# Mixing in a decoder block: epsilon, power, shift and store made per four tiles, the shift on VectorE

## The chip, the cores and the metric

The kernel runs on one core of a Trainium2 chip. The metric is device time of one execution in microseconds (us). Its engines are TensorE (PE, with its weight loads shown apart as PEld), VectorE (DVE), ScalarE (ACT), GpSimd (POOL) and SyncE (SP, which here only issues DMAs). Each engine runs its own instructions in order, and they wait for each other by semaphores.

## The reference, cut to what matters

The kernel is a decoder block on 64 sequences of 128 tokens with 128 features, all in float32: attention, cross attention and a soft mixture of experts, each followed by a residual and a layer normalisation. The change lies in the last part, where every token mixes the outputs of 64 experts with 32 slots each by a softmax over the experts.

```python
def _layernorm(x, axis=-1, eps=1e-05):
    m = jnp.mean(x, axis=axis, keepdims=True)
    v = jnp.var(x, axis=axis, keepdims=True)
    return (x - m) / jnp.sqrt(v + eps)
...
    logits = (jnp.einsum('tzd,ed->tze', x, phi_w) + phi_b).reshape(t, z, n, p)
    C = jax.nn.softmax(logits, axis=2)
    ...
    Y = jnp.einsum('tznp,npH->tzH', C, Y_tilde)
    return Y
...
x = _layernorm(x + _L0_ffn_ref(x, L0_ffn_phi_w, L0_ffn_phi_b, L0_ffn_expert_w, L0_ffn_expert_b), axis=-1)
```

## The kernel before

The program runs in blocks one after the other: setup, attention, cross attention, gathering the slots, the experts, and mixing. Mixing (mix_slots, L1261) begins at about 950 us of the span and lasts until its end. It handles 64 tiles of 128 tokens. The weights C of one tile are 128 tokens by 2048 (64 experts by 32 slots); they are made in two units of 1024 columns. For one tile:

- PE makes the logits of the first unit from six matmuls (L1200). Those of the second were kept in DRAM by an earlier block, and SP loads them into mix_read (L1192).
- DVE finds the largest logit per slot, of the first unit (mix_mx, L1227) and of the second (mix_high, L1231), and lowers one half of the first unit in PSUM (L1236); PE lowers its other half (L1206); POOL lowers the second unit (mix_less, L1249).
- ACT takes the exponentials of the first unit (L1215) and of the second (L1219). DVE sums each (mix_sums, L1241) and inverts the sums (mix_rinv, L1244). POOL multiplies each unit by them (mix_c, L1256).
- PE turns each unit (last_T, L1331), ACT copies it out of PSUM (last_cT, L1340), PE multiplies it with the slots' outputs (last_Y, L1324).
- The normalisation: DVE adds the residual (last_y, L1364) and takes mean and variance (L1367 to L1370); POOL adds epsilon, takes the power -0.5 and makes the shift, minus mean times the result (L1387, L1390, L1392), one column each; ACT makes the output, last_res, from y by this scale and shift (L1349); SP stores the outputs of two tiles with one DMA (L1304).

The order is written out by hand: every engine steps through k in ORDER, two steps to a tile, and a stage with lag n handles tile (k - n) / 2 in step k. In an even step DVE sums the second unit of one tile, finds the peaks of a later one and lowers it. In an odd step it does its part of the normalisation of the tile with lag 7 and then sums the first unit of the tile with lag 1. POOL divides two units in an even step and lowers one in an odd step, and then makes the three small values of the tile with lag 7. Two buffers of each kind are held in turn. reach() is a wait that is left out where its value is not above zero.

Of the kernel before, what the change touches and what calls it, by code (L numbers as in the profile page):

```python
# [55 lines left out]
def reach(eng, sem, value):  # L56

    if not isinstance(value, int) or value > 0:
        eng.wait_ge(sem, value)  # L59
# [1201 lines left out]
def mix_slots(nc, w, mix, out):  # L1261
# [5 lines left out]
    with ExitStack() as ctx:  # L1267
        st = Store(nc, ctx, "last")
        cT = [st.sb(f"cT{i}", [128, 8, 128]) for i in range(2)]
        y = [st.sb(f"y{i}", [128, 128]) for i in range(2)]  # L1270
        stats = st.sb("stats", [128, 6])
        mv = [st.sb(f"mv{i}", [128, 2]) for i in range(2)]
        veps = st.sb("veps", [128, 1])
        rstd = [st.sb(f"rstd{i}", [128, 1]) for i in range(2)]
        shift = [st.sb(f"shift{i}", [128, 1]) for i in range(2)]
        res = [st.sb(f"res{i}", [128, 2, 128]) for i in range(2)]
# [17 lines left out]
        ORDER = range(UNITS + 9)  # L1294

        @block.sync
        def _(sync):
            for t in range(TILES + 4):
                if t + READS - 1 < TILES:
                    mix.load(sync, t + READS - 1)  # L1300
                if t >= 4 and t % 2 == 0:
                    p = (t - 4) // 2
                    sync.wait_ge(res_ready, 2 * p + 2)
                    sync.dma_start(out[p * 256:(p + 1) * 256, :].rearrange("(b s) d -> s b d", b=2), res[p % 2][:])\  # L1304
                        .then_inc(stored[p % 2], 16)
            for i in range(2):
                sync.wait_ge(stored[i], 16 * (TILES // 4))
# [27 lines left out]
        def _(act):  # L1335
            for k in ORDER:
# [8 lines left out]
                for t in tiles(k, 8):  # L1345
                    act.wait_ge(shift_ready, t + 1)
                    if t >= 4:
                        act.wait_ge(stored[t // 2 % 2], 16 * (t // 4))
                    act.activation(res[t // 2 % 2][:, t % 2, :], y[t % 2][:], ACT.Identity, bias=shift[t % 2][:],  # L1349
                                   scale=rstd[t % 2][:]).then_inc(res_ready, 1)  # L1350

        @block.vector
        def _(dve):
            for k in ORDER:
# [3 lines left out]
                for t in tiles(k, 0):  # L1358
                    if t >= EARLY:
                        mix.peaks(dve, t)  # L1360
                for t in tiles(k, 7):
                    dve.wait_ge(cT_read, 2 * t + 2)
                    reach(dve, res_ready, t - 1)
                    dve.tensor_tensor(y[t % 2][:], psY[t % 2][:, 0:128], w.xres[:, t * 128:(t + 1) * 128], ALU.add)\  # L1364
                        .then_inc(y_done, 1)
                    dve.wait_ge(y_done, t + 1)
                    dve.bn_stats(stats[:], y[t % 2][:]).then_inc(st_done, 1)  # L1367
                    dve.wait_ge(st_done, t + 1)
                    dve.memset(w.scratch[:], 0.0)
                    dve.bn_aggr(mv[t % 2][:], stats[:]).then_inc(mv_ready, 1)  # L1370
# [5 lines left out]
        def _(pool):  # L1376
            for k in ORDER:
# [7 lines left out]
                for t in tiles(k, 7):  # L1385
                    pool.wait_ge(mv_ready, t + 1)
                    pool.tensor_tensor(veps[:], mv[t % 2][:, 1:2], w.eps[:, 0:1], ALU.add).then_inc(ve_done, 1)  # L1387
                    pool.wait_ge(ve_done, t + 1)
                    reach(pool, res_ready, t - 1)
                    pool.tensor_tensor(rstd[t % 2][:], veps[:], w.neg_half[:, 0:1], ALU.pow).then_inc(rstd_ready, 1)  # L1390
                    pool.wait_ge(rstd_ready, t + 1)
                    pool.tensor_scalar(shift[t % 2][:], mv[t % 2][:, 0:1], -1.0, rstd[t % 2][:], ALU.mult, ALU.mult)\  # L1392
                        .then_inc(shift_ready, 1)
# [104 lines left out]
```

## Time and profile before

| | us |
|---|---|
| median of 3 runs | 1399.61 (1399.18 to 1403.23) |
| the profiled execution's own time | 1401.92 |
| its span | 1399.9 |
| POOL busy in the span | 1180.2 (84%) |
| DVE busy | 1109.3 (79%) |
| PE busy, PE weight loads busy | 1293.0 (92%), 1055.0 (75%) |
| ACT busy | 896.6 (64%) |
| the chain that ended last: mix_c L1256, mix_less L1249 | 14%, 5% of the span |
| the same chain: last_rstd, last_shift, last_veps | 2%, 1%, 1% |

The span is that of one execution taken by the profiler, 2.0 us shorter than this execution's own time, which in turn is 2.3 us above the median. The shares are averages over all blocks. In the part of the span that mixing takes, the granted clock of PE is full, and PE, DVE and POOL are all busy for nine tenths or more, so that shares alone do not tell which of them sets the pace.

### The profile page before, as it was taken

How to read it: one execution, taken by the hardware profiler on the slowest of the kernel's cores; microseconds unless marked ns; L12 is line 12 of the kernel's file. 1: busy time of each engine (PE TensorE's matmuls, PEld its weight loads, DVE VectorE, ACT ScalarE, POOL GpSimd, SP SyncE). 2: the span in 40 equal slices, each digit the busy share in tenths (PEclk: the TensorE clock that was granted, in tenths of full speed). 3: DMA queues.
4: the chain of work that ended last, by engine and by line, in shares of the span. 5: the costliest groups of instructions: out<-in, count | busy, mean ns of one | idle time of the engine just before them, and what ended most of it. 6: DMA issues, size and time to landing. Idle time of an engine off the chain costs nothing. (4 is left out here: it accounts for less than half of the span.)

```text
span 1399.9 us, 31677 instructions
## 1 busy us (share of the span) xinstructions
PE 1293.0 (92%) x11006; PEld 1055.0 (75%) x11006; DVE 1109.3 (79%) x2462; ACT 896.6 (64%) x1670; POOL 1180.2 (84%) x1050
## 2 busy tenths in 40 slices
PE   4886789999999699999999999979999999999998
PEld 3664567777676477777777777748999999999997
DVE  4897456666666688888888888877999999999996
ACT  2897356666666476776776777735666666666664
POOL 7664568888888399999999999967999999999997
PEclk9998699999999999999999999999999999999999
DMA  5111243443443022222222222212222223232321
GB/s 167 47 40 55 84 134 117 121 122 115 125 121 94 24 84 89 92 83 91 91 84 90 91 87 87 84 48 94 84 88 83 88 84 89 82 91 80 92 79 31
DMA packets 83567, 123.61 MB, mean 88 GB/s; under 512 B 8593, under 2 KB 54226, under 8 KB 83410
## 3 DMA queue, kind: packets, MB, share of 16 engines
q1 hardware_dynamic: 81810, 117.16, 26.4%
q0 software_dynamic: 1088, 4.19, 1.0%
q8 instruction: 90, 1.47, 0.4%
q14 instruction: 67, 0.55, 0.1%
q10 hardware_dynamic: 512, 0.23, 0.1%
HBM read 70.28 MB, written 51.27 MB: 87 GB/s over the span
## 5 line engine op out<-in xcount | busy, mean ns | idle before, releaser
L997 POOL TENSOR_TENSOR gather_d<-gather_e,gather_rinv 128x1024 f32<-128x1024 f32 x128 | 244.8, 1913 | 36.6 <-DVE gather_rinv L976 36.5
L1256 POOL TENSOR_TENSOR mix_c<-mix_e,mix_rinv 128x1024 f32<-128x1024 f32 x128 | 240.9, 1902 | 18.7 <-DVE mix_rinv L1244 16.6
L1324 PEld LDWEIGHTS last_Y<-kept_phi,last_cT 128*128 128x128 f32 x2048 | 248.4, 192 | 7.3
L1324 PE MATMUL last_Y<-kept_phi,last_cT 128*128 128x128 f32 x2048 | 249.0, 275 | 0.0
L1340 ACT COPY last_cT<-last_T 128x1024 f32<-128x1024 f32 x128 | 128.4, 1003 | 132.1 <-PE last_T L1331 132.1
L822 POOL TENSOR_TENSOR cross_kd<-first_pack,kept_consts 128x624 fp32r<-128x624 f32 x128 | 155.6, 1237 | 63.7 <-DMA first_pack<-first_halves 54.1
L730 DVE TENSOR_REDUCE cross_mx<-cross_S 128x8 fp32r<-128x624 f32 x128 | 103.5, 809 | 113.0 <-PE cross_S L567 113.0
L1241 DVE TENSOR_REDUCE mix_sums<-mix_e 128x16 f32<-128x1024 f32 x128 | 155.8, 1217 | 34.4 <-ACT mix_e L1215 34.0
L972 DVE TENSOR_REDUCE gather_rsum<-gather_e 128x32 f32<-128x1024 f32 x128 | 156.1, 1220 | 25.9 <-ACT gather_e L945 25.9
L991 POOL TENSOR_TENSOR gather_dl<-gather_d,gather_dh 128x512 fp32r<-128x512 f32 x128 | 166.5, 1301 | 0.0
L934 ACT COPY gather_keep<-gather_L 128x256 f32<-128x256 f32 x256 | 94.7, 370 | 96.2 <-PE gather_L L908 95.9
L1331 PE MATMUL last_T<-kept_consts,mix_c 128*128 128x128 f32 x1024 | 134.2, 274 | 3.2 <-POOL mix_c L1256 1.1
L945 ACT ACTIVATE gather_e<-gather_L 128x1024 f32<-128x1024 f32 x128 | 131.1, 1024 | 7.5
L661 ACT ACTIVATE cross_pT<-cross_P 77x1024 f32<-77x1024 f32 x128 | 131.2, 1028 | 2.1 <-PE cross_P L587 2.1
L922 PE MATMUL slots_X<-gather_d,kept_xres 128*128 128x512 f32 x256 | 130.7, 592 | 0.0
L1249 POOL TENSOR_TENSOR mix_less<-mix_read,mix_high 128x1024 f32<-128x1024 f32 x64 | 122.5, 1914 | 7.4 <-DVE mix_high L1231 4.3
L1331 PEld LDWEIGHTS last_T<-kept_consts,mix_c 128*128 128x128 f32 x1024 | 114.6, 142 | 4.5 <-issue 2.5
L966 DVE TENSOR_REDUCE gather_mx<-gather_L 128x16 fp32r<-128x512 f32 x128 | 88.5, 691 | 30.3 <-PE gather_L L908 21.4
L927 PE MATMUL slots_X<-gather_dh,gather_x2h 128*128 128x512 f32 x128 | 101.0, 789 | 3.0 <-POOL gather_dl L991 3.0
L957 ACT CAST gather_dh<-gather_d 128x512 fp32r<-128x512 f32 x128 | 79.5, 621 | 31.6 <-PE slots_X L929 19.7
L968 DVE TENSOR_REDUCE gather_mx<-gather_L 128x16 fp32r<-128x512 f32 x128 | 87.0, 680 | 0.0
L908 PE MATMUL gather_L<-over_w1h,kept_xh 128*128 128x512 f32 x256 | 81.5, 400 | 4.3 <-ACT gather_e L945 3.3
(205 smaller groups left out, 3013.0 us busy)
## 6 DMA issues: line engine op xcount, KB each, us to landing
kept_logits<-gather_keep SPq DMA_DIRECT2D x128, 256.0 KB, 2.0
mix_read<-kept_logits SPq DMA_DIRECT2D x64, 512.0 KB, 3.7
first_halves<-first_qk SPq DMA_DIRECT2D x32, 412.0 KB, 3.0
first_pack<-first_halves SPq DMA_DIRECT2D x64, 128.0 KB
first_pack<-first_halves SPq DMA_DIRECT2D x32, 206.0 KB
first_pack<-first_halves SPq DMA_DIRECT2D x64, 78.0 KB
attn_xTg<-in_xT SPq DMA_DIRECT2D x16, 256.0 KB, 2.6
kept_xres<-in_x POOLq DMA_DIRECT2D x4, 1024.0 KB, 12.1
```

Of the source, the lines that this page charges most:

```text
L661: act.activation(pT[n % 2][0:J, hs, :, :], psP[:, hs, :, :], ACT.Exp)\
L822: pool.tensor_tensor(kd[n % 2][:, q], keys[:, q].to_broadcast([128, 2, 4, JP]), w.own.unsqueeze(1).unsqueeze(3).to_broadcast([128, 2, 4, J ...
L922: pe.matmul(psX[:, 2 * j + 1, :], w.xres[:, rows(u)], dd[u % 4][:, 1, :], start=first, stop=last)\
L945: act.activation(e[u % 2][:], psL[u % 2][:].rearrange("p i (n s) -> p i n s", n=16), ACT.Exp)\
L972: dve.tensor_reduce(rsum[u % 2][:].rearrange("p (i n) -> p i n", i=2), e[u % 2][:], X, ALU.add)\
L991: pool.tensor_tensor(dl[u % 2][:], dd[u % 4][:, 0, :], dh[u % 2][:], ALU.subtract).then_inc(dl_ready, 1)
L997: pool.tensor_tensor(dd[u % 4][:].rearrange("p i (n s) -> p i n s", n=16), e[u % 2][:], rinv[u % 2][:].rearrange("p (i n) -> p i n", i=2). ...
L1241: dve.tensor_reduce(self.sums[u % 2][:], self.e[u % 2][:], X, ALU.add).then_inc(self.sum_done, 1)
L1256: pool.tensor_tensor(self.cc[u % 2][:], self.e[u % 2][:], self.rinv[u % 2][:].unsqueeze(2).to_broadcast([128, 16, EXPERTS]), ALU.mult)\
L1324: ins = pe.matmul(psY[t % 2][:, 0:128], cT[u % 2][:, c, :], w.yk[:, 8 * (u % 2) + c, :], start=(u % 2 == 0 and c == 0), stop=(u % 2 == 1 a ...
L1331: ins = pe.transpose(psT[:, c, :], mix.cc[u % 2][:, 2 * c:2 * c + 2, :], w.ident)
L1340: act.copy(cT[u % 2][:], psT[:]).then_inc(cT_ready, 1)
```

## The change

The normalisation's small values are made once per four tiles. y, mean and variance of four tiles are collected in one of three buffers. POOL adds epsilon and takes the power on four columns, once in four tiles, and makes no shift. DVE makes the shift on four columns with one instruction, a scalar_tensor_tensor of mean and rstd, two steps after the power. ACT makes the outputs with lag 16 instead of 8. SP stores four tiles with one DMA.

```diff
--- before.py
+++ after.py
@@ -1267,13 +1267,13 @@
     with ExitStack() as ctx:
         st = Store(nc, ctx, "last")
         cT = [st.sb(f"cT{i}", [128, 8, 128]) for i in range(2)]
-        y = [st.sb(f"y{i}", [128, 128]) for i in range(2)]
+        y = [st.sb(f"y{i}", [128, 4, 128]) for i in range(3)]
         stats = st.sb("stats", [128, 6])
-        mv = [st.sb(f"mv{i}", [128, 2]) for i in range(2)]
-        veps = st.sb("veps", [128, 1])
-        rstd = [st.sb(f"rstd{i}", [128, 1]) for i in range(2)]
-        shift = [st.sb(f"shift{i}", [128, 1]) for i in range(2)]
-        res = [st.sb(f"res{i}", [128, 2, 128]) for i in range(2)]
+        mv = [st.sb(f"mv{i}", [128, 4, 2]) for i in range(3)]
+        veps = st.sb("veps", [128, 4])
+        rstd = [st.sb(f"rstd{i}", [128, 4]) for i in range(3)]
+        shift = [st.sb(f"shift{i}", [128, 4]) for i in range(3)]
+        res = [st.sb(f"res{i}", [128, 4, 128]) for i in range(2)]
         psT = st.ps("T", [128, 8, 128])
         psY = [st.ps(f"Y{i}", [128, 512]) for i in range(2)]
 
@@ -1291,20 +1291,24 @@
 
             return [(k - lag) // 2] if (k - lag) % 2 == 0 and 0 <= k - lag < UNITS else []
 
-        ORDER = range(UNITS + 9)
+        def fours(k, lag):
+
+            return [t // 4 for t in tiles(k, lag) if t % 4 == 3]
+
+        ORDER = range(UNITS + 15)
 
         @block.sync
         def _(sync):
-            for t in range(TILES + 4):
+            for t in range(TILES + 12):
                 if t + READS - 1 < TILES:
                     mix.load(sync, t + READS - 1)
-                if t >= 4 and t % 2 == 0:
-                    p = (t - 4) // 2
-                    sync.wait_ge(res_ready, 2 * p + 2)
-                    sync.dma_start(out[p * 256:(p + 1) * 256, :].rearrange("(b s) d -> s b d", b=2), res[p % 2][:])\
+                if t >= 12 and t % 4 == 0:
+                    p = (t - 12) // 4
+                    sync.wait_ge(res_ready, 4 * p + 4)
+                    sync.dma_start(out[p * 512:(p + 1) * 512, :].rearrange("(b s) d -> s b d", b=4), res[p % 2][:])\
                         .then_inc(stored[p % 2], 16)
             for i in range(2):
-                sync.wait_ge(stored[i], 16 * (TILES // 4))
+                sync.wait_ge(stored[i], 16 * (TILES // 8))
 
         @block.tensor
         def _(pe):
@@ -1342,12 +1346,13 @@
                     if t >= 1:
                         mix.exponentials(act, t, 0)
                         mix.exponentials(act, t, 1)
-                for t in tiles(k, 8):
-                    act.wait_ge(shift_ready, t + 1)
-                    if t >= 4:
-                        act.wait_ge(stored[t // 2 % 2], 16 * (t // 4))
-                    act.activation(res[t // 2 % 2][:, t % 2, :], y[t % 2][:], ACT.Identity, bias=shift[t % 2][:],
-                                   scale=rstd[t % 2][:]).then_inc(res_ready, 1)
+                for t in tiles(k, 16):
+                    p, i = t // 4, t % 4
+                    if i == 0:
+                        act.wait_ge(shift_ready, p + 1)
+                        reach(act, stored[p % 2], 16 * (p // 2))
+                    act.activation(res[p % 2][:, i, :], y[p % 3][:, i, :], ACT.Identity, bias=shift[p % 3][:, i:i + 1],
+                                   scale=rstd[p % 3][:, i:i + 1]).then_inc(res_ready, 1)
 
         @block.vector
         def _(dve):
@@ -1358,16 +1363,21 @@
                 for t in tiles(k, 0):
                     if t >= EARLY:
                         mix.peaks(dve, t)
+                for p in fours(k, 9):
+                    dve.wait_ge(rstd_ready, p + 1)
+                    dve.scalar_tensor_tensor(out=shift[p % 3][:], in0=mv[p % 3][:, :, 0], scalar=-1.0, in1=rstd[p % 3][:],
+                                             op0=ALU.mult, op1=ALU.mult).then_inc(shift_ready, 1)
                 for t in tiles(k, 7):
+                    p, i = t // 4, t % 4
                     dve.wait_ge(cT_read, 2 * t + 2)
-                    reach(dve, res_ready, t - 1)
-                    dve.tensor_tensor(y[t % 2][:], psY[t % 2][:, 0:128], w.xres[:, t * 128:(t + 1) * 128], ALU.add)\
+                    reach(dve, res_ready, 4 * (p - 2))
+                    dve.tensor_tensor(y[p % 3][:, i, :], psY[t % 2][:, 0:128], w.xres[:, t * 128:(t + 1) * 128], ALU.add)\
                         .then_inc(y_done, 1)
                     dve.wait_ge(y_done, t + 1)
-                    dve.bn_stats(stats[:], y[t % 2][:]).then_inc(st_done, 1)
+                    dve.bn_stats(stats[:], y[p % 3][:, i, :]).then_inc(st_done, 1)
                     dve.wait_ge(st_done, t + 1)
                     dve.memset(w.scratch[:], 0.0)
-                    dve.bn_aggr(mv[t % 2][:], stats[:]).then_inc(mv_ready, 1)
+                    dve.bn_aggr(mv[p % 3][:, i, :], stats[:]).then_inc(mv_ready, 1)
                 for t in tiles(k, 1):
                     if t >= 1:
                         mix.invert_sums(dve, 2 * t)
@@ -1382,15 +1392,12 @@
                 for t in tiles(k, 1):
                     if t >= 1:
                         mix.lower(pool, t)
-                for t in tiles(k, 7):
-                    pool.wait_ge(mv_ready, t + 1)
-                    pool.tensor_tensor(veps[:], mv[t % 2][:, 1:2], w.eps[:, 0:1], ALU.add).then_inc(ve_done, 1)
-                    pool.wait_ge(ve_done, t + 1)
-                    reach(pool, res_ready, t - 1)
-                    pool.tensor_tensor(rstd[t % 2][:], veps[:], w.neg_half[:, 0:1], ALU.pow).then_inc(rstd_ready, 1)
-                    pool.wait_ge(rstd_ready, t + 1)
-                    pool.tensor_scalar(shift[t % 2][:], mv[t % 2][:, 0:1], -1.0, rstd[t % 2][:], ALU.mult, ALU.mult)\
-                        .then_inc(shift_ready, 1)
+                for p in fours(k, 7):
+                    pool.wait_ge(mv_ready, 4 * p + 4)
+                    pool.tensor_tensor(veps[:], mv[p % 3][:, :, 1], w.eps[:, 0:4], ALU.add).then_inc(ve_done, 1)
+                    pool.wait_ge(ve_done, p + 1)
+                    reach(pool, res_ready, 4 * (p - 2))
+                    pool.tensor_tensor(rstd[p % 3][:], veps[:], w.neg_half[:, 0:4], ALU.pow).then_inc(rstd_ready, 1)
 
 
 class Weights:
```

On POOL, in the middle of mixing, the program before has this order for two tiles; last_veps, last_rstd and last_shift are the three small values, mix_c the two products, mix_less the lowered unit.

```order
L1256 TENSOR_TENSOR mix_c<-mix_e,mix_rinv 128x1024 x2
L1249 TENSOR_TENSOR mix_less<-mix_read,mix_high 128x1024
L1387 TENSOR_TENSOR last_veps<-last_mv,kept_eps 128x1
L1390 TENSOR_TENSOR last_rstd<-last_veps,kept_neg_half 128x1
L1392 TENSOR_SCALAR last_shift<-last_mv,last_rstd 128x1
L1256 TENSOR_TENSOR mix_c<-mix_e,mix_rinv 128x1024 x2
L1249 TENSOR_TENSOR mix_less<-mix_read,mix_high 128x1024
```

And the changed program, over four tiles:

```order
L1249 TENSOR_TENSOR mix_less<-mix_read,mix_high 128x1024
L1397 TENSOR_TENSOR last_veps<-last_mv,kept_eps 128x4
L1400 TENSOR_TENSOR last_rstd<-last_veps,kept_neg_half 128x4
L1256 TENSOR_TENSOR mix_c<-mix_e,mix_rinv 128x1024 x2
L1249 TENSOR_TENSOR mix_less<-mix_read,mix_high 128x1024
L1256 TENSOR_TENSOR mix_c<-mix_e,mix_rinv 128x1024 x2
L1249 TENSOR_TENSOR mix_less<-mix_read,mix_high 128x1024
L1256 TENSOR_TENSOR mix_c<-mix_e,mix_rinv 128x1024 x2
L1249 TENSOR_TENSOR mix_less<-mix_read,mix_high 128x1024
L1256 TENSOR_TENSOR mix_c<-mix_e,mix_rinv 128x1024 x2
L1249 TENSOR_TENSOR mix_less<-mix_read,mix_high 128x1024
```

Three of four tiles have no small values on POOL any more; in the fourth there are two instead of three, of four columns.

On DVE, between the lowering of the first unit (slots_X) and the sum of the next first unit (mix_sums), the program before has:

```order
L1231 TENSOR_REDUCE mix_high<-mix_read 128x16
L1236 TENSOR_TENSOR slots_X<-slots_X,mix_mx 128x512
L1364 TENSOR_TENSOR last_y<-last_Y,kept_xres 128x128
L1367 BN_STATS last_stats<-last_y 128x6
L1369 MEMSET kept_scratch 128x1
L1370 BN_AGGR last_mv<-last_stats 128x2
L1241 TENSOR_REDUCE mix_sums<-mix_e 128x16
L1244 RECIPROCAL mix_rinv<-mix_sums 128x16
```

The changed program has there, once in four tiles:

```order
L1231 TENSOR_REDUCE mix_high<-mix_read 128x16
L1236 TENSOR_TENSOR slots_X<-slots_X,mix_mx 128x512
L1368 SCALAR_TENSOR_TENSOR last_shift<-last_mv,last_rstd 128x4
L1374 TENSOR_TENSOR last_y<-last_Y,kept_xres 128x128
L1377 BN_STATS last_stats<-last_y 128x6
L1379 MEMSET kept_scratch 128x1
L1380 BN_AGGR last_mv<-last_stats 128x2
L1241 TENSOR_REDUCE mix_sums<-mix_e 128x16
L1244 RECIPROCAL mix_rinv<-mix_sums 128x16
```

The new last_shift stands ahead of last_y, so it comes right behind the lowering; in the other three tiles the order is as before.

On ACT, at the end of the program, before:

```order
L1215 ACTIVATE mix_e<-slots_X 128x1024
L1219 ACTIVATE mix_e<-mix_less 128x2x16x32
L1340 COPY last_cT<-last_T 128x1024
L1349 ACTIVATE last_res<-last_y,last_shift,last_rstd 128x128
L1340 COPY last_cT<-last_T 128x1024 x2
L1349 ACTIVATE last_res<-last_y,last_shift,last_rstd 128x128 x3
```

And changed:

```order
L1215 ACTIVATE mix_e<-slots_X 128x1024
L1219 ACTIVATE mix_e<-mix_less 128x2x16x32
L1344 COPY last_cT<-last_T 128x1024
L1354 ACTIVATE last_res<-last_y,last_shift,last_rstd 128x128
L1344 COPY last_cT<-last_T 128x1024 x2
L1354 ACTIVATE last_res<-last_y,last_shift,last_rstd 128x128 x7
```

Seven outputs instead of three stand behind the last copy; the last four of them wait for one shift.

## Rows read from the trace of the kernel before

**Rows 1.** Waits, 960 to 1385 us: us in total, times, longest us.

```profile
DVE mix_sums L1241 <- ACT mix_e L1215: 28.6, 62, 1.7
...
POOL mix_c L1256 <- DVE mix_rinv L1244: 10.7, 46, 1.9
```

**Rows 2.** Timeline, DVE, two tiles: start, us, instruction, idle before it.

```profile
1242.82 0.28 DVE L1364 TENSOR_TENSOR last_y<-last_Y,kept_xres 128x128 f32<-128x128 f32 x1
...
1244.08 1.22 DVE L1241 TENSOR_REDUCE mix_sums<-mix_e 128x16 f32<-128x1024 f32 x1 [0.44 <-ACT mix_e L1215]
1245.33 0.25 DVE L1244 RECIPROCAL mix_rinv<-mix_sums 128x16 f32<-128x16 f32 x1
1245.59 1.22 DVE L1241 TENSOR_REDUCE mix_sums<-mix_e 128x16 f32<-128x1024 f32 x1
...
1249.82 0.28 DVE L1364 TENSOR_TENSOR last_y<-last_Y,kept_xres 128x128 f32<-128x128 f32 x1
...
1251.08 1.22 DVE L1241 TENSOR_REDUCE mix_sums<-mix_e 128x16 f32<-128x1024 f32 x1 [0.43 <-ACT mix_e L1215]
```

**Rows 3.** Timeline, POOL, the same two tiles.

```profile
1238.77 3.76 POOL L1256 TENSOR_TENSOR mix_c<-mix_e,mix_rinv 128x1024 f32<-128x1024 f32 x2 [0.23 <-DVE mix_rinv L1244]
1242.50 1.91 POOL L1249 TENSOR_TENSOR mix_less<-mix_read,mix_high 128x1024 f32<-128x1024 f32 x1
1244.37 0.18 POOL L1387 TENSOR_TENSOR last_veps<-last_mv,kept_eps 128x1 f32<-128x1 f32 x1
...
1245.67 3.76 POOL L1256 TENSOR_TENSOR mix_c<-mix_e,mix_rinv 128x1024 f32<-128x1024 f32 x2
1249.39 1.92 POOL L1249 TENSOR_TENSOR mix_less<-mix_read,mix_high 128x1024 f32<-128x1024 f32 x1
```

**Rows 4.** Timeline, ACT, the two exponentials of one tile.

```profile
1243.02 1.03 ACT L1215 ACTIVATE mix_e<-slots_X 128x1024 f32<-128x1024 f32 x1 [0.15 <-DVE slots_X L1236]
1244.50 1.06 ACT L1219 ACTIVATE mix_e<-mix_less 128x1024 f32<-128x1024 f32 x1 [0.45 <-POOL mix_less L1249]
```

**Rows 5.** Timeline, DVE and POOL together, early in attention.

```profile
18.13 6.95 POOL L214 MEMSET kept_xl<- 32x8192 f32 x1
...
21.05 4.32 DVE L352 TENSOR_SCALAR attn_band<-attn_a 128x512 f32<-128x512 f32 x1 [1.31 <-ACT attn_a L325]
```

**Rows 6.** One line, L352: shortest, median and longest duration in ns.

```profile
L352 DVE TENSOR_SCALAR attn_band<-attn_a x16: 426/427/4315, 21.0 to 118.4; 128x512 f32<-128x512 f32 x16
```

**Rows 7.** Timeline, the last tiles of gathering.

```profile
909.60 1.28 POOL L991 TENSOR_TENSOR gather_dl<-gather_d,gather_dh 128x512 fp32r<-128x512 f32 x1
...
912.98 1.45 POOL L991 TENSOR_TENSOR gather_dl<-gather_d,gather_dh 128x512 fp32r<-128x512 f32 x1
...
913.08 0.23 DVE L982 TENSOR_TENSOR gather_x2l<-kept_xres,gather_x2h 128x128 fp32r<-128x128 f32 x1
```

**Rows 8.** Timeline, POOL: epsilon and power on four columns, in the experts.

```profile
930.72 0.20 POOL L1082 TENSOR_TENSOR expert_veps<-expert_mv,kept_eps 128x4 f32<-128x4 f32 x1 [1.18 <-DVE expert_mv L1044]
931.00 1.01 POOL L1084 TENSOR_TENSOR expert_rstd<-expert_veps,kept_neg_half 128x4 f32<-128x4 f32 x1
```

**Rows 9.** One line, L231: the power on four columns in attention, ns.

```profile
L231 POOL TENSOR_TENSOR attn_rstd<-attn_veps,kept_neg_half x16: 1006/1408/1427, 44.4 to 134.4; 128x4 f32<-128x4 f32 x16
```

**Rows 10.** Timeline, the last tile: power and output.

```profile
1395.53 0.55 POOL L1390 TENSOR_TENSOR last_rstd<-last_veps,kept_neg_half 128x1 f32<-128x1 f32 x1
...
1396.47 0.49 ACT L1349 ACTIVATE last_res<-last_y,last_shift,last_rstd 128x128 f32<-128x128 f32 x1 [3.92 <-POOL last_shift L1392]
```

**Rows 11.** Timeline, attention: shift on DVE and four outputs on ACT.

```profile
135.46 0.16 DVE L361 SCALAR_TENSOR_TENSOR attn_shift<-attn_mv,attn_rstd 128x4 f32<-128x4 f32 x1 [1.39 <-POOL attn_rstd L231]
135.66 1.65 ACT L309 ACTIVATE kept_xres<-attn_y,attn_shift,attn_rstd 128x128 f32<-128x128 f32 x4 [2.48 <-DVE attn_shift L361]
```

**Rows 12.** DMA issues: KB each, median us from issue to landing.

```profile
kept_logits<-gather_keep SPq DMA_DIRECT2D x128, 256.0 KB, 2.0
...
out<-last_res SPq DMA_DIRECT2D x32, 128.0 KB, 1.8
```

## The prediction

> **What bounds the kernel now.** I read the page first. Its chain that ended last runs along POOL, through the divisions, the lowering and the three small values, and POOL is the busiest engine of mixing after PE. Taken by itself that says: take work off POOL and the tile gets shorter. So I went to the waits of mixing and then to the timelines of two tiles in its middle. DVE waits for the first exponential 62 times, 28.6 us in all, and POOL's division waits for DVE's reciprocal in 46 places [rows 1]. In the timelines a tile lasts 6.90 or 7.00 us in turn: the divisions start at 1238.77 and 1245.67 [rows 3], the first sums at 1244.08 and 1251.08 [rows 2].
>
> Where the profile names no wait before a division (1245.67), DVE's reciprocal ended at 1245.33 + 0.25 = 1245.58, 0.09 before it [rows 2, 3]. So POOL had nothing to start earlier with there either; its small values end just in time. What closes the loop is DVE with ACT: DVE lowers the first unit, ACT takes 1.03 us for the exponential from 1243.02 [rows 4], DVE sums it from 1244.08 (1243.02 + 1.03 = 1244.05), inverts, sums the second unit, finds the peaks, lowers the next. In this loop DVE idles 0.43 to 0.44 us a tile and only there [rows 2]; that idle time does not depend on POOL. A second loop, over two tiles, does pass POOL: the reciprocal, two divisions (3.76), mix_less (1.91), the second exponential from 1244.50 for 1.06 to 1245.56, the second sum at 1245.59 [rows 2 to 4]. It delays every second tile by about 0.1, which makes the turn of 6.90 and 7.00. The small values are no part of it either: they stand behind mix_less and ahead of the division, in time that POOL has while it waits for the reciprocal.
>
> **What the change removes.** On POOL, three small values in three tiles of four. From the start of veps to the division they take 1245.67 - 1244.37 = 1.30 us [rows 3]. By the reading above the division still starts 0.09 behind the reciprocal, so this buys nothing in time: after it POOL waits longer for DVE. In the fourth tile POOL has two instructions of four columns: 0.28 from the start of veps to the power, 1.01 for the power [rows 8], and some 0.1 to the division, 1.39 against 1.30. I take the 1.01 of the experts; in attention the power took up to 1.41 [rows 9], where DVE instructions ran beside it. The division then comes 0.1 later once in four tiles (0.5 with 1.41), and half of the tiles have 0.1 to spare. I count it with the next term.
>
> SP's stores, half as many, wait for outputs that are made later, and no longer stand ahead of a load that could be issued. Nothing waits for those loads now, so this is nothing. ACT's outputs keep their place in the even step, behind the copy; the shift they need is made a step before, so nothing too. y and its statistics go to a larger buffer, same instructions. The outputs that free a buffer of y are done some four tiles before it is written again.
>
> **What it adds: the shift on DVE.** It takes 0.16 us [rows 11], once in four tiles, and stands right behind the lowering and ahead of y. Behind it on DVE are y, the statistics and then the first sum, which has the 0.44 of idle time in front. If the shift just ran, 0.16 would vanish in 0.44. But look at what POOL does at that place: mix_less runs from 1242.50 to 1244.41, and y starts at 1242.82, in the next tile from 1249.39 to 1251.31 and at 1249.82 [rows 2, 3]. The shift falls 0.32 to 0.43 behind the start of a POOL instruction that streams 1024 elements a partition out of SBUF. It has two operands in SBUF, mean and rstd. The DVE instructions that stand beside POOL's divisions and mix_less now (the reductions, the lowering in PSUM, y from PSUM and the residual, the reciprocal) have at most one; so the profile of mixing cannot show what two do there.
>
> Elsewhere rows tell of it. In attention a DVE tensor_scalar that began at 21.05 took 4.32 us, until 0.29 us behind the end of POOL's memset (18.13 + 6.95 = 25.08) [rows 5]; its median is 0.427 [rows 6]. DVE was held by a POOL instruction that had begun. This one has one input, so it is not the shift's form. With two inputs in SBUF there is gathering: DVE's x2l began 0.10 behind a POOL subtraction; DVE took its 0.23, and POOL 1.45 where the one before took 1.28 [rows 7]. So the two engines exclude each other with two inputs as well, and there DVE was first in line. No row has such an instruction starting in the middle of POOL's. The bounds are therefore: not held at all, 0 (hidden in the idle 0.44); DVE gets in first and mix_less grows by about 0.17, as in rows 7; held until mix_less ends. I take the last, since the nearest row for the order "POOL first" is rows 5, and 0.32 to 0.43 is well behind 0.10.
>
> The Trainium skill (SBUF — State Buffer, Who interferes with whom) has a rule for it that speaks against this change: a DVE instruction with two SBUF inputs contends with a GpSimd instruction that reads SBUF, and whichever issues first keeps the shared pair for the whole instruction. By that rule the sum is the one below; without it, 1401.4 us. The trace agrees as far as rows 5 and 7 go, and no run here shows the two-input case held.
>
> Price of one hold: y starts at 1244.41 instead of 1242.82. From y to the sum DVE needs 1244.08 - 1242.82 - 0.44 = 0.82, so the sum starts at 1245.23 instead of 1244.08, 1.15 later. In the other kind of tile: 1251.31 + (1251.08 - 1249.82 - 0.43) = 1252.14 instead of 1251.08, 1.06 later. The mean is 1.10, and mix_less of that tile itself is up to 0.1 later by the longer power, so 1.15. It is lost in full: DVE's own loop sets the pace, POOL waits behind it. There are 16 groups; the last group's shift comes after the last mix_less, so 15 x 1.15 = 17.3 us.
>
> **The end.** After the last y: the power takes 1.01 instead of 0.55 (+0.46) [rows 8, 10]; the shift is about even; ACT makes four outputs behind one shift, 1.65 instead of 0.49 (+1.16) [rows 10, 11]; the store has 256 KB instead of 128, 2.0 against 1.8 us to landing (+0.2) [rows 12]. Together +1.8.
>
> Sum: 17.3 + 1.8 = 19.1. The profiled execution took 1401.92 us (span 1399.9), so it becomes 1421.0; the median of the runs is 2.3 lower, and there I forecast 1399.61 + 19.1 = 1418.7 us.
>
> **Rivals.**
> - *The shift is not held* (a hold applies to other forms only, or DVE gets in first). For it: x2l ran freely at 0.10 behind POOL's start, and the shift is only 0.2 to 0.3 later than that; four elements are little. Against it: rows 5. Time: the end's 1.8 alone, 1401.4; with mix_less growing by 0.17 in each of 15 groups, up to 2.5 more, 1403.9. Not slower, within what can be told. It decides by whether POOL has the path already at 0.3 us behind its start. 19%.
> - *Some are held, or the power takes attention's time.* If half of the groups are held, 8 x 1.15 + 1.8 gives 1410.6; if none is and the power takes 1.41, the division of that tile is 0.4 later and 15 x 0.4 + 1.8 gives 1407.4. Slower. 8%.
> - *POOL sets the pace after all*, as its chain says, and DVE follows by using up its idle time. For it: the chain, and that POOL ends its small values within 0.1 of the reciprocal. Against: the exponential's 1.03 lies between two DVE instructions whatever POOL does. At most the whole 28.6 us of rows 1 could go: 1399.6 - 28.6 + 1.8 = 1372.8; a third of it would give 1391.9. 7%.
> - *Forecast*, held in about all groups: 66%, own range 1413 to 1424 (power of 1.41 and a later mix_less add up to 15 x 0.4 = 6 us).
>
> **How the numbers follow.** Two runs of this kernel can be told apart at about 0.3%, 4.2 us. The forecast and the second rival are slower by more: 74%. The first rival is within 0.3%, nearly all of it: 19%. The last is faster: 7%. The range reaches from the lower end of the first rival, 1401, to the upper end of the forecast, 1424; outside lie the last rival, and a little at both edges.
>
> **What would show it.** In the changed profile last_shift on DVE would take some 1.5 us or y start about 1.6 behind the lowering, ending with mix_less, 15 times; its wait-free time of 0.16 would appear only in the last group. DVE's first sum would lose its idle time before it in these tiles, tiles would last 6.9, 7.0, 6.9 and 8.1, and POOL would wait for mix_rinv in every tile, over 1 us in three of four. If last_shift stays at 0.16 with y right behind it, the forecast is wrong and the first rival right. If the tiles without a group's work get shorter than 6.9, my reading of the loop is wrong.

## The result

The changed kernel takes 1412.83 us (median of 5 runs, 1408.37 to 1413.52), the kernel before 1399.61 beside it. The ratio is 1.0087, with a 95% interval of 1.0065 to 1.0108: slower, by some 13 us. The profiled execution took 1413.52 us, with a span of 1411.7.

| us | before | after |
|---|---|---|
| span | 1399.9 | 1411.7 |
| POOL busy in the span | 1180.2 | 1138.5 |
| DVE busy | 1109.3 | 1127.9 |
| first sum of tile 3 to first sum of tile 63 (60 tiles of mixing) | 965.74 to 1383.42: 417.7 | 963.54 to 1394.12: 430.6 |
| start of the last y to the end of the span | 1394.34: 5.6 | 1405.00: 6.7 |

These 60 tiles take 12.9 us longer and the end 1.1; what lies ahead of the first sum of tile 3 was 2.2 shorter in this execution. That last number has two parts: the blocks ahead of mixing, which the change does not touch, were 3.5 shorter (the first lowering of the first unit starts at 932.11 instead of 935.59), and the first tiles of mixing took 1.3 longer. 12.9 + 1.1 - 2.2 is the 11.8 us between the spans. POOL lost 42 us of work and the kernel became slower.

### The profile page after: what moved, and what is told of

Its sections match the earlier page's. It is cut to its first block and busy times, and to the rows that moved or that the text cites. A ratio compares the mean times of both kernels' runs of the same rounds, so it can differ in the third digit from the quotient of the medians.

```text
span 1411.7 us, 31412 instructions
## 1 busy us (share of the span) xinstructions
PE 1297.2 (92%) x11006; PEld 1056.5 (75%) x11006; DVE 1127.9 (80%) x2478; ACT 897.1 (64%) x1670; POOL 1138.5 (81%) x890
```

## The profile after

The new instruction first: one line of the changed kernel, with shortest, median and longest duration in ns.

```profile
L1368 DVE SCALAR_TENSOR_TENSOR last_shift<-last_mv,last_rstd x16: 164/1502/1585, 990.1 to 1407.2; 128x4 f32<-128x4 f32 x16
```

The same instruction took 152 to 164 ns in all 16 executions of attention. Here the median is 1502; the one of 164 is the last group's. Now the timeline of DVE around one of them; columns as in [rows 2], to which these answer.

```profile
1206.97 1.22 DVE L1241 TENSOR_REDUCE mix_sums<-mix_e 128x16 f32<-128x1024 f32 x1 [0.44 <-ACT mix_e L1215]
...
1213.87 1.22 DVE L1241 TENSOR_REDUCE mix_sums<-mix_e 128x16 f32<-128x1024 f32 x1 [0.44 <-ACT mix_e L1215]
...
1219.02 0.69 DVE L1236 TENSOR_TENSOR slots_X<-slots_X,mix_mx 128x512 f32<-128x512 f32 x1
1219.62 1.50 DVE L1368 SCALAR_TENSOR_TENSOR last_shift<-last_mv,last_rstd 128x4 f32<-128x4 f32 x1
1221.04 0.28 DVE L1374 TENSOR_TENSOR last_y<-last_Y,kept_xres 128x128 f32<-128x128 f32 x1
...
1221.78 1.19 DVE L1241 TENSOR_REDUCE mix_sums<-mix_e 128x16 f32<-128x1024 f32 x1
...
1228.60 1.22 DVE L1241 TENSOR_REDUCE mix_sums<-mix_e 128x16 f32<-128x1024 f32 x1 [0.44 <-ACT mix_e L1215]
```

And POOL over the same tiles, answering to [rows 3] and [rows 8].

```profile
1208.56 3.76 POOL L1256 TENSOR_TENSOR mix_c<-mix_e,mix_rinv 128x1024 f32<-128x1024 f32 x2 [1.38 <-DVE mix_rinv L1244]
...
1214.15 0.20 POOL L1397 TENSOR_TENSOR last_veps<-last_mv,kept_eps 128x4 f32<-128x4 f32 x1
1214.44 1.01 POOL L1400 TENSOR_TENSOR last_rstd<-last_veps,kept_neg_half 128x4 f32<-128x4 f32 x1
1215.45 3.77 POOL L1256 TENSOR_TENSOR mix_c<-mix_e,mix_rinv 128x1024 f32<-128x1024 f32 x2
1219.18 1.91 POOL L1249 TENSOR_TENSOR mix_less<-mix_read,mix_high 128x1024 f32<-128x1024 f32 x1
1223.33 3.77 POOL L1256 TENSOR_TENSOR mix_c<-mix_e,mix_rinv 128x1024 f32<-128x1024 f32 x2 [2.24 <-DVE mix_rinv L1244]
```

The shift starts at 1219.62, 0.44 behind mix_less, and lasts until 1221.12; mix_less ends at 1219.18 + 1.91 = 1221.09. y follows at 1221.04, where it would have stood at 1219.62 before. The idle 0.44 in front of the first sum is gone in this tile, and the tile from 1213.87 to 1221.78 lasts 7.91. Four tiles, from one held shift's first sum to the next, last 7.91, 6.83, 7.04 and 6.90, together 28.68; before, 417.7 / 60 x 4 = 27.85.

The power of four columns takes 1.01 and ends as the next division starts, 1215.45. DVE's reciprocal there (1215.12 for 0.25) ends at 1215.37, 0.08 before, and a division that waits for nothing else starts 0.08 behind the reciprocal too (1208.23 + 0.25 = 1208.48, division at 1208.56). So the power costs nothing. Where POOL has no small values it just waits: 1.38 us at 1208.56, 2.24 behind a held shift. The waits of mixing show the same in sum (us, times, longest), against 28.6 and 10.7 in [rows 1]:

```profile
POOL mix_c L1256 <- DVE mix_rinv L1244: 73.8, 46, 2.3
...
DVE mix_sums L1241 <- ACT mix_e L1215: 19.7, 45, 0.5
PEld last_T L1335 <- POOL mix_c L1256: 12.3, 15, 0.9
```

POOL's wait for the reciprocal rose from 10.7 to 73.8 us: the work taken off POOL turned into waiting. TensorE's weight load now waits for POOL's product, 15 times, once behind each hold. The end, against [rows 10, 11]:

```profile
1406.20 1.01 POOL L1400 TENSOR_TENSOR last_rstd<-last_veps,kept_neg_half 128x4 f32<-128x4 f32 x1
```

```profile
1407.24 0.16 DVE L1368 SCALAR_TENSOR_TENSOR last_shift<-last_mv,last_rstd 128x4 f32<-128x4 f32 x1 [1.40 <-POOL last_rstd L1400]
```

```profile
1407.44 1.65 ACT L1354 ACTIVATE last_res<-last_y,last_shift,last_rstd 128x128 f32<-128x128 f32 x4 [3.84 <-DVE last_shift L1368]
```

## Experiments

The theory is that a DVE instruction with two tensor inputs in SBUF is held until a POOL instruction that reads SBUF, and had begun before it, has ended. The rivals: that the place or the wait for rstd delays it; that the grouping itself costs; that DVE loses to POOL wherever they meet; that a scalar_tensor_tensor is held whatever its inputs are. Ratios are to the kernel before, with 95% intervals.

**The instruction alone, put into the kernel before.**

```diff
+                    if 4 <= t and t % 4 == 0:
+                        dve.scalar_tensor_tensor(out=spare[:], in0=w.eps[:, 0:4], scalar=-1.0, in1=w.neg_half[:, 0:4],
+                                                 op0=ALU.mult, op1=ALU.mult)
                     dve.wait_ge(cT_read, 2 * t + 2)
```

> The kernel before with one instruction added on VectorE ahead of y in one tile of four (15 times): a scalar_tensor_tensor of two constant 4-column tiles in SBUF into a spare tile that nobody reads, with no wait. Theory: it is held by mix_less for 1.5 us each time and costs what the holds of the changed kernel cost, 15 x 0.88 = 13: 1413. Rival (the cost lies in the grouping or in the wait for rstd, not in the instruction): its 0.16 vanishes in the idle time: 1400.

Measured: 1411.66 us, ratio 1.0093 (1.0074 to 1.0113), what the whole change costs. The added line, in ns:

```profile
L1364 DVE SCALAR_TENSOR_TENSOR last_spare<-kept_eps,kept_neg_half x15: 1496/1504/1612, 987.6 to 1389.9; 128x4 f32<-128x4 f32 x15
```

No wait, constant inputs, nobody reads its output, and nothing is grouped: only the instruction's form and place are left as the cause. Its tiles have the changed kernel's turn of 7.92, 6.83, 7.05, 6.90.

**The same in every tile.** The condition is t >= 1.

> The same added instruction on VectorE in every tile from the second on (63 instead of 15). Theory: every one is held, and nothing is given back between them: a tile of 7.8 to 7.9 instead of 6.95, 61 x 0.9 = 55 above before: 1454. Rival (the pipeline absorbs most of it once all tiles are alike): under 1430.

Measured: 1454.76 us, ratio 1.0399 (1.0380 to 1.0419), as expected. The tiles last 7.88 throughout. The median of the added instruction is now 1.65 us, since DVE comes to it 0.28 behind the start of mix_less instead of 0.43 or 0.44:

```profile
L1364 DVE SCALAR_TENSOR_TENSOR last_spare<-kept_eps,kept_neg_half x63: 130/1652/1658, 969.9 to 1444.3; 128x4 f32<-128x4 f32 x63
```

The price per hold hardly changes: 0.86 us in the changed kernel with 15 (12.9 / 15), 0.88 in the kernel of the first experiment ((1411.7 - 1398.5) / 15), and 0.91 here with 62 ((1454.8 - 1398.3) / 62; the last of the 63 took 0.13). Two of the 62 stand at the end, where no mix_less is left. They meet POOL's two divisions:

```profile
1438.66 3.76 POOL L1256 TENSOR_TENSOR mix_c<-mix_e,mix_rinv 128x1024 f32<-128x1024 f32 x2 [0.21 <-DVE mix_rinv L1244]
```

```profile
1439.86 0.72 DVE L1364 SCALAR_TENSOR_TENSOR last_spare<-kept_eps,kept_neg_half 128x4 f32<-128x4 f32 x1
...
1441.24 1.19 DVE L1364 SCALAR_TENSOR_TENSOR last_spare<-kept_eps,kept_neg_half 128x4 f32<-128x4 f32 x1
```

A division takes 1.90, so the first ends at 1440.56 and the second at 1442.42; the held instructions end at 1440.58 and 1442.43. So the same instruction lasts 0.72, 1.19, 1.50 or 1.65 us, by what is left of the POOL instruction that is running, and divisions hold it like mix_less.

**The same shift with one tensor input.**

```diff
-                    dve.scalar_tensor_tensor(out=shift[p % 3][:], in0=mv[p % 3][:, :, 0], scalar=-1.0, in1=rstd[p % 3][:],
-                                             op0=ALU.mult, op1=ALU.mult).then_inc(shift_ready, 1)
+                    for i in range(4):
+                        ins = dve.tensor_scalar(shift[p % 3][:, i:i + 1], mv[p % 3][:, i, 0:1], -1.0,
+                                                rstd[p % 3][:, i:i + 1], ALU.mult, ALU.mult)
+                    ins.then_inc(shift_ready, 1)
```

> The shift stays on VectorE at the same place with the same wait, but as four tensor_scalar instructions of one column, with one tensor in SBUF each (rstd is a scalar operand). Theory (two tensor inputs in SBUF are what is held): no hold, each takes below 0.1 and all lie in the idle 0.44; only the end's 1.2 and perhaps 0.1 a group from the power remain: 1401 to 1403. Rival (any VectorE instruction at this place waits, for rstd or for POOL): the first of the four takes 1.5 and the time stays at 1413.

Measured: 1399.52 us, ratio 1.0008 (0.9995 to 1.0021): the cost is gone. DVE, timeline of the same place:

```profile
1212.57 0.69 DVE L1236 TENSOR_TENSOR slots_X<-slots_X,mix_mx 128x512 f32<-128x512 f32 x1
1213.17 0.57 DVE L1369 TENSOR_SCALAR last_shift<-last_mv,last_rstd 128x1 f32<-128x1 f32 x4
1213.65 0.29 DVE L1376 TENSOR_TENSOR last_y<-last_Y,kept_xres 128x128 f32<-128x128 f32 x1
...
1214.44 1.22 DVE L1241 TENSOR_REDUCE mix_sums<-mix_e 128x16 f32<-128x1024 f32 x1
```

POOL's mix_less runs there from 1212.78 to 1214.69, and the four instructions, each some 0.2 us with overlap, go through beside it: 0.57 us for all, in the idle time. Place, wait and grouping are those of the changed kernel, so each of the rivals that name them falls. I had expected below 0.1 us each; they took more and it did not matter.

This run changes the operation together with the number of inputs. Attention, in the kernel before, takes the two apart: its attn_y is a scalar_tensor_tensor too, but with one of its two tensors in PSUM (attn_O) and one in SBUF.

```profile
46.77 1.27 POOL L222 TENSOR_TENSOR attn_band<-attn_band 128x512 f32<-128x512 f32 x1 [0.98 <-DVE attn_band L357]
```

```profile
47.69 1.13 DVE L384 SCALAR_TENSOR_TENSOR attn_y<-attn_O,attn_rinv,kept_xres 128x128 f32<-128x128 f32 x4
```

```profile
L384 DVE SCALAR_TENSOR_TENSOR attn_y<-attn_O,attn_rinv,kept_xres x64: 339/342/353, 41.6 to 132.4; 128x128 f32<-128x128 f32 x64
```

The first of these four starts 0.92 behind a POOL instruction that reads two tensors in SBUF and has 0.35 left. In 19 of the 64 cases attn_y starts 0.45 to 1.08 behind the start of such an instruction of POOL, with 0.19 or more of it left, and all 64 take 339 to 353 ns. So it is not the operation that is held, but the operation with both tensors in SBUF.

**The same instruction at another place.** It goes from ahead of y to behind the first reciprocal.

```diff
                 for t in tiles(k, 1):
                     if t >= 1:
                         mix.invert_sums(dve, 2 * t)
+                for p in fours(k, 9):
+                    dve.wait_ge(rstd_ready, p + 1)
+                    dve.scalar_tensor_tensor(out=shift[p % 3][:], in0=mv[p % 3][:, :, 0], scalar=-1.0, in1=rstd[p % 3][:],
...
```

> The same single shift instruction with two inputs in SBUF, moved behind the reciprocal of the first sum, which releases POOL's division 0.09 later. Theory (who comes first keeps the port): VectorE is first there, the shift takes its 0.16 and POOL's division grows by up to 0.17, as gather_x2l did to the subtraction; 15 x (0.07 to 0.2) and 1.2 at the end: 1402 to 1404. Rival (VectorE loses whenever POOL runs): it is held through the division, 1.7 us each time and on the path: 1425.

Measured: 1399.36 us, ratio 0.9997 (0.9983 to 1.0011), where 1402 to 1404 was expected. DVE and then POOL:

```profile
1239.48 0.25 DVE L1244 RECIPROCAL mix_rinv<-mix_sums 128x16 f32<-128x16 f32 x1
1239.65 0.10 DVE L1382 SCALAR_TENSOR_TENSOR last_shift<-last_mv,last_rstd 128x4 f32<-128x4 f32 x1
1239.72 1.22 DVE L1241 TENSOR_REDUCE mix_sums<-mix_e 128x16 f32<-128x1024 f32 x1
```

```profile
1239.82 3.76 POOL L1256 TENSOR_TENSOR mix_c<-mix_e,mix_rinv 128x1024 f32<-128x1024 f32 x2 [1.29 <-DVE mix_rinv L1244]
```

The two-input shift starts 0.17 us ahead of the division and takes 0.10 us, so it is over before the division starts, and the division is not longer than elsewhere (3.76 for two). That is why my 1402 to 1404 did not come: the two never meet. What the run shows is that the form alone does not cost anything; it is held only where a POOL instruction is already running. A repair of the change is to move four lines. That DVE keeps its place when POOL arrives while the two-input instruction is still running is not shown by it. The nearest rows are [rows 7], the one case of 64 in gathering, and attention in the kernel before, where attn_f reads two tensors in SBUF and POOL takes its power of four columns:

```profile
123.10 0.29 DVE L401 CUSTOM_DVE_ANT_0 attn_f<-attn_band,attn_a 128x128 f32<-128x128 f32 x1
...
123.53 0.28 DVE L401 CUSTOM_DVE_ANT_0 attn_f<-attn_band,attn_a 128x128 f32<-128x128 f32 x1
```

```profile
123.31 1.16 POOL L231 TENSOR_TENSOR attn_rstd<-attn_veps,kept_neg_half 128x4 f32<-128x4 f32 x1
```

DVE's instructions take 0.28 to 0.29, as where POOL is idle beside them, though the last starts 0.22 behind POOL's, and POOL's takes 1.16 instead of the 1.01 that it takes in the last two groups of attention, with no attn_f beside it. So a two-input instruction is not held by every POOL instruction with an earlier recorded start; which part of a POOL instruction holds was not tried.

**The shift on POOL.** The product of mean and rstd and a change of sign follow the power there.

```diff
+                    pool.tensor_tensor(prod[:], mv[p % 3][:, :, 0], rstd[p % 3][:], ALU.mult).then_inc(prod_done, 1)
+                    pool.wait_ge(prod_done, p + 1)
+                    pool.tensor_scalar(shift[p % 3][:], prod[:], -1.0, None, ALU.mult).then_inc(shift_ready, 1)
```

> The shift of four columns is made by POOL (a product and a change of sign, behind the power) and not by VectorE; all else as in the changed kernel. Theory (VectorE is held by mix_less): the 15 holds go, with their 0.88 us a group; POOL's division comes later once in four tiles, by 1.39 + 0.56 - 1.30, some 0.65 us, of which the two-tile loop passes on all or all but 0.1: 15 x 0.6 = 8, and 1.5 at the end, so about 1409, and above all VectorE has its 0.44 of idle time before every first sum. Rival (the grouping itself costs: buffers, late outputs, one store for four tiles): the time stays at 1413 and beyond it by the added 8, 1421.

Measured: 1407.16 us, ratio 1.0057 (1.0041 to 1.0073); 1409 was expected. The holds are gone, but four small values in a row reach past the reciprocal, and the division comes late: the four tiles last 7.11, 7.26, 6.89 and 7.01, together 28.27, 0.42 more than before. From the start of veps to the division POOL now takes 1.87 instead of 1.30; of these 0.57 more, 0.42 are paid.

**DVE's loop opened.** My account of before says that DVE and the exponential close a loop. To test it, mix_high and mix_less are made one tile ahead. The part of peaks() that makes mix_high becomes a function of its own, kept_peaks(). Then mix_high stands behind the lowering and covers the exponential.

```diff
                     if t >= EARLY:
                         mix.peaks(dve, t)
+                        if t + 1 < TILES:
+                            mix.kept_peaks(dve, t + 1)
...
                 for t in tiles(k, 1):
-                    if t >= 1:
-                        mix.lower(pool, t)
+                    if t == 1:
+                        mix.lower(pool, 1)
+                    if t >= 1 and t + 1 < TILES:
+                        mix.lower(pool, t + 1)
```

This goes on the kernel before:

> The kernel before with mix_high and mix_less of a tile made one tile earlier, so that mix_high stands behind VectorE's lowering of the first unit and covers ScalarE's exponential; the small values stay on POOL per tile. Theory (VectorE with the exponential sets the pace, POOL's own loop of 3.73 + 1.91 + 1.30 = 6.94 lies just below): VectorE's idle 0.44 goes, but POOL is then the bound at 6.94: no change, 1398 to 1400. Rival (POOL never was near a bound): down to TensorE's 6.7 a tile, 1386.

on the one-input kernel:

> The same reordering on the kernel with grouped small values and the shift as four one-input instructions. Theory: POOL is relieved to 5.64 a tile (7.0 in one of four) and VectorE to 6.5, so TensorE is next with some 6.7 a tile: 61 x 0.23 = 14 less, 1.2 more at the end: 1386. Here the removed POOL work is worth something. Rival (another loop closes at 6.9): 1399.

and on the changed kernel:

> The same reordering on the changed kernel itself, with the two-input shift at its place behind the lowering. Theory: the shift is still held until mix_less ends, 1.5 us once in four tiles, but VectorE now has slack of its own: 3 x 6.5 + 7.9 = 27.4 for four tiles instead of 28.7: 1394. Rival (the hold costs its 0.88 on top of TensorE's 6.7 a tile): 1386 + 13 = 1399.

Measured: 1405.47 (1.0044, 1.0030 to 1.0057), 1405.94 (1.0054, 1.0038 to 1.0070) and 1405.13 us (1.0046, 1.0032 to 1.0060). The two gains I expected did not come, and the first was expected to stay at 1400. The start of mixing is longer in these kernels: from the first lowering of the first unit to the first sum of tile 3 it takes 35.2 us in the first two and 32.7 in the third, 30.2 before; what makes it longer was not tried. After it the tiles of the first last 6.94 and 7.01 in turn, and POOL's own instructions fill 6.94, and those of the second 6.93, and 7.14 once in four. What holds them at 6.93 is TensorE: its product, turn, lowering, product, turn and logits follow each other without a gap. PE's instructions of one tile in the second kernel (the last row, of the next tile, is cut off by the edge of the window):

```profile
1203.50 1.95 PE L1331 MATMUL last_Y<-kept_phi,last_cT 128*128 128x128 f32 x16
1205.29 1.04 PE L1338 MATMUL last_T<-kept_consts,mix_c 128*128 128x128 f32 x8
1206.08 0.46 PE L1206 MATMUL slots_X<-mix_mx,kept_neg_ident 128*128 128x512 f32 x1
1206.38 1.95 PE L1331 MATMUL last_Y<-kept_phi,last_cT 128*128 128x128 f32 x16
1208.16 1.04 PE L1338 MATMUL last_T<-kept_consts,mix_c 128*128 128x128 f32 x8
1208.95 0.71 PE L1200 MATMUL slots_X<-over_w2h,kept_xh 128*128 128x512 f32 x2
1209.50 0.63 PE L1200 MATMUL slots_X<-over_w2h,kept_xl 128*128 128x512 f32 x2
1209.97 0.62 PE L1200 MATMUL slots_X<-over_w2l,kept_xh 128*128 128x512 f32 x2
1210.44 0.83 PE L1331 MATMUL last_Y<-kept_phi,last_cT 128*128 128x128 f32 x6
```

From 1203.50 to 1210.44 is 6.94, and each group starts before the one ahead of it has ended. My 6.7 for TensorE was too low.

The third kernel shows something more. I had expected the shift to be held there too. Its median is 154 ns:

```profile
L1375 DVE SCALAR_TENSOR_TENSOR last_shift<-last_mv,last_rstd x16: 152/154/1264, 992.3 to 1398.0; 128x4 f32<-128x4 f32 x16
```

```profile
1215.83 0.15 DVE L1375 SCALAR_TENSOR_TENSOR last_shift<-last_mv,last_rstd 128x4 f32<-128x4 f32 x1
```

```profile
1212.18 3.76 POOL L1259 TENSOR_TENSOR mix_c<-mix_e,mix_rinv 128x1024 f32<-128x1024 f32 x2
1215.99 1.92 POOL L1252 TENSOR_TENSOR mix_less<-mix_read,mix_high 128x1024 f32<-128x1024 f32 x1
```

The shift stands at the same place of the code, but POOL is later in these tiles: behind the power it is still in its second division, until 1212.18 + 3.76 = 1215.94, and mix_less follows at 1215.99. The shift starts 0.12 before that division ends and ends at 1215.98, 0.03 to 0.04 behind the end and before mix_less starts. So it did not come first here; it met only the last tenth of a microsecond of a POOL instruction. Its 0.15 is what it takes in attention with POOL idle, so whether it waited at all can't be told. The longest, 1264 ns, is the group in which it started 0.66 behind the second division's start, with 1.25 of it left. How long the shift is held is set by what is left of POOL's instruction, and 14 of these 16 came as one was about to end.

**TensorE relieved.** The third product of the logits is left out, so that the output lacks the correction by xh with w2l. TensorE does 0.47 us less per tile.

```diff
-        for n, (xs, ws) in enumerate(((w.xh, w.w2h), (w.xl, w.w2h), (w.xh, w.w2l))):
+        for n, (xs, ws) in enumerate(((w.xh, w.w2h), (w.xl, w.w2h))):
...
-                                start=n == 0, stop=n == 2)
+                                start=n == 0, stop=n == 1)
```

> The kernel before without the third product of the logits (xh with w2l), so two of eight wide TensorE matmuls a tile are left out, 0.47 us a tile; the output lacks that correction. Theory (three things lie at 6.9 to 7.0 a tile: VectorE with the exponential, the two-tile loop, and TensorE's own 6.93): no change in mixing, at most 2 us less, 1396 to 1399. Rival (TensorE alone sets the pace): 6.5 a tile, 1370.

> The same product left out of the kernel with one-input shift and mix_high a tile ahead, where VectorE no longer waits for its lowering and POOL is relieved. Theory (there TensorE is the only bound left at 6.93): down by most of 0.47 a tile until VectorE's 6.5 or ScalarE closes: 61 x 0.35 = 21 less than its 1406, so 1385. Rival (its 6.93 comes from the chain of mix_c, last_T, last_cT and the exponential): no change, 1404.

> The same product left out of the changed kernel. Theory (VectorE with the holds sets 28.7 us for four tiles, TensorE only waits): 1411 to 1413 as the changed kernel. Rival (TensorE runs 0.9 behind after a hold and its own 6.93 for the other tiles makes the price of 0.88): part of the cost goes, 3 x 0.1 to 3 x 0.2 a group, 1405 to 1408.

Measured: 1397.87 (0.9989, 0.9976 to 1.0001), 1397.03 (0.9988, 0.9973 to 1.0003) and 1413.32 us (1.0093, 1.0069 to 1.0117). The first: nothing, so TensorE alone does not set the pace before. In its trace TensorE now waits for POOL's product in 57 tiles (980 to 1380 us):

```profile
PEld last_T L1331 <- POOL mix_c L1256: 26.4, 57, 0.8
DVE mix_sums L1241 <- ACT mix_e L1215: 25.6, 58, 0.7
```

and the turn of 6.89 and 7.02 stays. The second: 8.9 us below the 1405.94 of the kernel it is made from, less than the 21 expected. Three tiles of four fall to 6.65, less than the whole 0.47, and what holds them there was not tried. The fourth, where POOL takes the power, rises to 7.42. The third is as slow as the changed kernel, with the same 7.91, 6.82, 7.04, 6.90, so TensorE has no part in the price of a hold.

## Why the prediction was right

**What bounds the kernel.** The reading that POOL's small values stand beside the path was right: they went, and POOL's waits grew by 63 us. The loop of DVE and ACT was right as far as it went. What I left out is that TensorE's own 6.93 us a tile lies at the same height, so three bounds meet within 0.1 us: DVE with the exponential 6.90, the two-tile loop through mix_less 6.95, TensorE 6.93. The kernels with mix_high ahead showed it: TensorE's work less by 0.47 a tile gains nothing where the two loops through DVE stand (1397.9), and brings 6.93 down to 6.65 in three of four tiles where mix_high ahead has opened them. The two loops themselves, 6.90 and 6.95, are read from the rows; no run takes one away and leaves the other. It changed nothing in this forecast.

**The hold.** Right in mechanism, place and count: 15 held, one free, and y released with the end of mix_less. The size was off: 17.3 forecast, 12.9 measured. In parts, by the tile shown above: the holds fell on the kind of tile with mix_less 0.44 ahead, for which I had y 1.49 late and the sum 1.06; y is 1.42 late, as it starts 0.05 before mix_less's recorded end. From y to the sum DVE needs 0.74, not 0.82. So the sum is 1.42 + 0.74 - 1.26 = 0.90 late, where I had a mean of 1.10. The 0.05 for a later mix_less was nothing, since the power ends just in time. The rest, to 12.9 / 15 = 0.86, comes back in the next tiles, which last 6.83 and 7.04 instead of 6.90 and 7.01. In the first of them DVE's sums take 1.19 and 1.16, where they took 1.22 and 1.20 in the tile from 1206.97; why, no run tells.

**The end.** 1.8 forecast, 1.1 measured. The power at 1.01, the shift at 0.16 and the outputs at 1.65 are as in the rows. I had the shift as about even, but from the start of the power to the outputs it is 1407.44 - 1406.20 = 1.24 instead of 1396.47 - 1395.53 = 0.94, so of the power's 0.46 the shorter shift gives 0.16 back. From the last output to the end of the span it is 1411.7 - 1409.09 = 2.6 instead of 1399.9 - 1396.96 = 2.9, so the larger store did not add 0.2; this part became 0.3 shorter. Why, no run tells. Over all tiles a store's median from issue to landing rose from 1.8 to 4.5 us, not to the 2.0 that I took from a DMA of equal size; nothing waits for it in mixing.

**The rule.** Of the Trainium skill's rule (SBUF — State Buffer, Who interferes with whom) no row showed before that a DVE instruction with two inputs in SBUF is held by a POOL instruction that reads SBUF. That is shown now: mix_less and the divisions hold it (1502 ns; 0.72 and 1.19), and with one input in SBUF it is not held (0.57 us for four; attn_y). The other half, that DVE keeps its place where it comes first, rests on rows alone, as said above: in my runs the shift had ended before POOL's instruction began. The rival that the shift slips in at 0.3 to 0.4 behind POOL's start fell in all 15 cases.

**The row that I rested the choice on.** I took "held until mix_less ends" because of [rows 5], and wrote that the trace agrees with the rule as far as rows 5 and 7 go. Rows 5 are another case: DVE's instruction there has one input in SBUF, and POOL's is a memset, which reads nothing. By the rule as I gave it that is no instance, and one-input instructions of one column ran freely beside mix_less. So rows 5 pointed the right way without being a case of what happened: by the rows alone the choice was lucky, and what speaks for it is the rule. What held the one-input instruction of 512 columns was not tried.

**The other rivals.** POOL as the pace fell with its 73.8 us of waiting; "some are held, or a power of 1.41" fell with the durations: 15 of 15, and 1.01.

**What did not come out** as the prediction's last part said: the tiles are 7.91 rather than 8.1, the one after a hold is 6.83, and POOL waits for mix_rinv in three tiles of four and not in every tile (46 times from 960 to 1385 us): where it takes the power, it ends just in time.

## What to carry to other kernels

An instruction of 0.16 us moved to another engine can cost more than five times its length (0.86), if it has two tensor inputs in SBUF and starts while POOL is in a long instruction that reads SBUF. Two ways out worked here: small instructions with one tensor input and a scalar operand (128x1), or a place where DVE comes to it while POOL is idle. One input is not a pass in general: the tensor_scalar of 128x512 in [rows 5] has one and was held for 4.32 us. Before taking work off the busiest engine, look at what releases the instruction behind that work; where that is another engine's result 0.1 us before, the relief becomes a wait. An idle gap on DVE is cover only for work that is really done in its own time there.

## What the hardware showed that I had not expected

- A hold goes by POOL's instruction and not by the data of DVE's: four columns were held for 0.72, 1.19, 1.26, 1.50 or 1.65 us, and end 0.01 to 0.03 behind POOL's instruction. Where POOL is idle, the same instruction takes 0.10 to 0.16.
- The shift at 0.10 us behind the reciprocal is shorter than the 0.15 to 0.16 that the same form took in attention and in the last group; what makes the difference was not tried.
- Where the shift came ahead, POOL's instruction was not longer for it (mix_less 1.92, two divisions 3.76), unlike the subtraction in [rows 7]. The shift had ended when they began (1239.75 against 1239.82, 1215.98 against 1215.99), and x2l had not.
